# A fused attention and feed-forward kernel: ScalarE's and TensorE's order at the seam behind each feed-forward stage is rewritten

## The reference

```python
xh = layernorm(x)
u = einsum(q, k) * scale / sqrt(16)          # q from xh, k and v from ctx, by head
p = softmax(where(mask, -inf, tanh(u) * exp(log_C)))
x = x + (p @ v) @ W_out.T
out = layernorm(x); gf = global_net(out.mean over tokens)     # 256 -> 128 -> 64 -> 1
for _ in range(3):
    tf = sigmoid(gelu(gelu(gelu(out @ w1 + b1) @ w2 + b2) @ w3 + b3) @ w4 + b4)
    coupling = 0.1 + adaptive_range * (0.7 * gf + 0.3 * tf - 0.5) * 2
    out = out + coupling * twist(out)        # twist permutes quarters of the features, with signs
x = x + out
```

## Time and profile before

| | us |
|---|---|
| median of 3 runs | 1056.2 (1056.09 to 1056.72) |
| the profiled execution: its own time | 1056.83 |
| its span, first to last instruction | 1055.0 |
| from one seam to the next (token_tanh at 296.65 and 421.77) | 125.1 |
| TensorE, ScalarE, VectorE, GpSimd busy | 972.8, 902.8, 819.0, 603.8 |

### The profile page before, as it was taken

The page is one execution under the profiler, slowest core; times in us unless marked ns, Lnnn a source line. Parts: engine busy times, 40 slices in busy tenths (PEclk is TensorE's granted clock), DMA queues, the critical chain, the costliest instruction groups (busy, mean ns, idle before and its releaser), DMA issues.

```text
span 1055.0 us, 21747 instructions
## 1 busy us (share of the span) xinstructions
PE 972.8 (92%) x7260; PEld 529.1 (50%) x7260; DVE 819.0 (78%) x1655; ACT 902.8 (86%) x1121; POOL 603.8 (57%) x1077
## 2 busy tenths in 40 slices
PE   5899999999999999999999999999999999997994
PEld 4556535564356544565445653556435654454431
DVE  3888785997869876887859978599786987687475
ACT  3899878997899978998789988899789997896575
POOL 3366715887069850898328980588706975087204
PEclk7999999999999999999999999999999999999897
DMA  5433001540024300332005310154002430021002
GB/s 119 89 60 60 6 2 31 117 90 1 2 69 91 78 1 1 90 93 56 2 1 119 89 30 1 32 117 90 0 2 70 94 75 1 1 52 37 8 1 81
DMA packets 191117, 51.70 MB, mean 49 GB/s; under 512 B 165920, under 2 KB 174624, under 8 KB 191008
## 3 DMA queue, kind: packets, MB, share of 16 engines
q1 hardware_dynamic: 191008, 50.31, 22.5%
HBM read 33.37 MB, written 16.78 MB: 48 GB/s over the span
## 4 chain that ended last, share of the span: by engine, by line
PE 41%; ACT 36%; issue 10%; DVE 8%; POOL 3%; SPq 2%; DMA 0%; ACTq 0%; DVEq 0%; POOLq 0%
ACT probs L939 17%; ACT probs L945 13%; PE ps L1295 11%; PE ps L1281 8%; PE ps L1265 6%; ACT f_t L955 4%; PE ps L1304 4%; PE ps L1185 4%; PE ps L1216 3%; DVE move_u L802 2%; DVE move_v L804 2%; PE ps L1201 2%; DVE f_t L808 2%; PE ps L1325 1%; SPq L412 1%
## 5 line engine op out<-in xcount | busy, mean ns | idle before, releaser
L939 ACT ACTIVATE probs<-ps,u_scale 120x2048 f32<-120x2048 f32 x128 | 258.0, 2016 | 23.0 <-PE ps L1185 23.0
L945 ACT ACTIVATE probs<-probs,exp_bias,clip 120x2048 f32<-120x2048 f32 x128 | 275.6, 2153 | 0.1
L1295 PE MATMUL ps<-h,w 128*128 128x512 f32 x384 | 186.9, 609 | 1.7 <-ACT h L973 1.7
L1185 PE MATMUL ps<-q_t,k_t 32*120 32x256 f32 x2048 | 148.3, 403 | 26.7 <-ACT probs L939 25.9
L717 DVE STREAM_TRANSPOSE o_t<-ps 128x512 f32<-128x512 f32 x128 | 90.6, 708 | 73.6 <-PE ps L1201 73.4
L1216 PE MATMUL ps<-wo_t,of_t 128*128 128x256 f32 x512 | 143.5, 403 | 1.0 <-DVE xy L742 1.0
L1201 PE MATMUL ps<-probs,va 120*32 120x256 f32 x2048 | 138.8, 389 | 1.3 <-ACT probs L945 1.3
L498 POOL TENSOR_SCALAR tok_c<-tok_c,c_tok 128x32 f32<-128x32 f32 x8 | 2.3, 288 | 237.7 <-issue 237.7
L1185 PEld LDWEIGHTS ps<-q_t,k_t 32*120 32x120 f32 x2048 | 93.8, 179 | 63.8 <-issue 59.5
L973 ACT ACTIVATE h<-f_t,b 128x512 f32<-128x512 f32 x144 | 96.9, 718 | 18.0 <-DVE f_t L827 13.5
L1216 PEld LDWEIGHTS ps<-wo_t,of_t 128*128 128x128 f32 x512 | 86.9, 189 | 50.0 <-issue 41.7
(11 more groups left out here) (138 smaller groups left out, 1765.5 us busy)
## 6 DMA issues: line engine op xcount, KB each, us to landing
xy<-in_x_dram SPq DMA_DIRECT2D x64, 256.0 KB, 3.4
out_dram<-xy SPq DMA_DIRECT2D x64, 256.0 KB, 2.0
cbuf<-in_ctx_dram SPq DMA_DIRECT2D x64, 120.0 KB, 2.8
va<-in_ctx_dram SPq DMA_DIRECT2D x64, 120.0 KB, 3.6
tok_c<-coup SPq DMA_DIRECT2D x256, 0.5 KB, 2.0
move_v<-in_L_xattn_W_out_dram SPq DMA_DIRECT2D x1, 256.0 KB, 5.1
move_u<-in_L_ffn_cn_w_dram SPq DMA_DIRECT2D x1, 256.0 KB, 3.1
w<-in_L_ffn_cn_w_dram SPq DMA_DIRECT2D x1, 128.0 KB, 3.0
```

What stands on the lines that cost most here:

```text
L939: eng.activation(probs[:, b % 2, n * HALF:(n + 1) * HALF, :].rearrange("k h q -> k (h q)"), banks(SCORE_BANK, 4)[0:KEYS, :], ACT.Tanh, sca ...
L945: eng.activation(p, p, ACT.Exp, scale=clip[0:KEYS, 0:1], bias=exp_bias[:, b:b + 1]).then_inc(s_exp, 1)
L1185: last = eng.matmul(banks(SCORE_BANK + r)[0:KEYS, odd * S:(odd + 1) * S], k_t[rows, b % 2, odd, n, :], q_t[rows, b % 2, n, :], start=True, ...
L1295: last = eng.matmul(banks(bank), w2[:, k, :], h1[:, p % 2, k, :], start=(k == 0), stop=(k == EK - 1))
```

## The change

1. On TensorE norm_to_features(24) moves from slot 27 into the ffn loop (p = 11), to `SIDE_BANK`; scores(27, 1) moves one step later, behind layer3(11); token_output(10) moves behind it, and token_output writes `X_BANK`. weighted_values(26, 0) leaves the ffn loop for slot 27.
2. TensorE's slot 27 becomes queries(28), weighted_values(26, 0), keys(28), project(25, 0), scores(28, 0), weighted_values(26, 1), project(25, 1). Slot 28 no longer begins with scores(28, 0).
3. ScalarE's order becomes gelu2(11), gelu3(10), features(24), gelu3(11), tanh(27, 1), token_tanh, exp(27, 0), and slot 28 as before.
4. VectorE does queries_out(28) ahead of attn_out(26, 0).
5. queries(28) waits for the last gelu3 in place of token_tanh; project(25, 0) waits for token_tanh in place of the last wide tanh.

In the last group, behind which no attention follows, only the order of token_output(10) and layer3(11), and the bank of the token outputs, change.

```diff
@@ vector
+                    if after_ffn(i) and nxt < NB:
+                        queries_out(nxt)
                     if 0 <= here < NB:
                         attn_out(here, 0)
-                    if 0 <= nxt < NB:
+                    if 0 <= nxt < NB and not after_ffn(i):
                         queries_out(nxt)
@@ scalar, attention slot
-                    if 0 <= i - LAG < NB:
-                        features(i - LAG)
+                    if 0 <= i - LAG < NB and not first:
+                        features(i - LAG, TR_BANK)
@@ scalar, ffn loop
-                            if early < NB and p >= PASSES - 2 and p < PASSES:
-                                tanh(early, p - PASSES + 2)
+                            if early < NB:
+                                if p == PASSES - 2:
+                                    tanh(early, 0)
+                                if p == PASSES - 1:
+                                    features(early - LAG, SIDE_BANK)
+                                if p == PASSES:
+                                    tanh(early, 1)
@@ tensor, queries(b)
                 elif after_ffn(b - 1):
-                    eng.wait_ge(s_ttok, groups_before(b - 1))
+                    eng.wait_ge(s_h3, PASSES * groups_before(b - 1))
@@ tensor, project(b, 0)
                     if after_ffn(b + 2):
-                        eng.wait_ge(s_th, UPDATES * groups_before(b + 2))
+                        eng.wait_ge(s_ttok, groups_before(b + 2))
@@ tensor, norm_to_features(b, bank)
-                if nxt < NB:
+                if bank == SIDE_BANK:
+                    eng.wait_ge(s_h2, PASSES * groups_before(b + LAG))
+                elif nxt < NB:
                     eng.wait_ge(s_kt, nxt + 1)
@@ tensor, attention slot
                     if i != early:
-                        if 0 <= i < NB:
+                        if 0 <= i < NB and i - 1 != early:
                             scores(i, 0)
...
                     else:
-                        if old < NB:
-                            project(old, 0)
-                        if nxt < NB:
-                            queries(nxt)
-                        if here < NB:
-                            weighted_values(here, 1)
-                    if 0 <= nxt < NB:
+                        queries(nxt)
+                        weighted_values(here, 0)
                         keys(nxt)
-                    if 0 <= here < NB and i != early:
+                        project(old, 0)
+                        scores(nxt, 0)
                         weighted_values(here, 1)
-                    if 0 <= old < NB:
                         project(old, 1)
-                    if 0 <= i - LAG < NB:
-                        norm_to_features(i - LAG)
@@ tensor, ffn loop
-                        if p - 2 >= UPDATES:
+                        if p - 2 >= UPDATES and p < PASSES:
                             token_output(i, p - 2)
...
                             if p == PASSES - 2:
                                 scores(early, 0)
                             if p == PASSES - 1:
+                                norm_to_features(early - LAG, SIDE_BANK)
+                            if p == PASSES:
                                 scores(early, 1)
-                            if p == PASSES:
-                                weighted_values(early - 1, 0)
+                        if p >= PASSES:
+                            token_output(i, p - 2)
```

More of the change, by code:

```diff
@@ L199, in xattn_ffn_kernel @@
         SMALL_AT = S
-        TOKEN_AT = S + 32
+        TOKEN_BANK = X_BANK
         L4_BANK = X_BANK
@@ L945, in exp, with features @@
                 eng.activation(p, p, ACT.Exp, scale=clip[0:KEYS, 0:1], bias=exp_bias[:, b:b + 1]).then_inc(s_exp, 1)
-            def features(b):
+            def features(b, bank):
                 eng.wait_ge(s_ftr, b + 1)
@@ L954, in features @@
                 for k in range(EK):
-                    eng.activation(f_t[:, k, at * S:(at + 1) * S], banks(TR_BANK)[:, k * S:(k + 1) * S],
+                    eng.activation(f_t[:, k, at * S:(at + 1) * S], banks(bank)[:, k * S:(k + 1) * S],
                                    ACT.Identity, scale=F_SCALE, accum_out=f_sum[:, k, at:at + 1]).then_inc(s_ft, 1)
@@ L1026, in token_tanh @@
                 eng.wait_ge(s_coef, COEFS * g)
-                eng.activation(tok_th[:], banks(TR_BANK)[:, TOKEN_AT:TOKEN_AT + GT], ACT.Tanh, scale=0.5,
+                eng.activation(tok_th[:], banks(TOKEN_BANK)[:, 0:GT], ACT.Tanh, scale=0.5,
                                bias=half_b4[:, 0:1]).then_inc(s_ttok, 1)
@@ L1218, in project, with norm_to_features @@
                 last.then_inc(s_proj, 1)
-            def norm_to_features(b):
+            def norm_to_features(b, bank):
                 eng.wait_ge(s_fhat, 2 * (b + 1))
                 nxt = b + LAG + 1
-                if nxt < NB:
+                if bank == SIDE_BANK:
+                    eng.wait_ge(s_h2, PASSES * groups_before(b + LAG))
+                elif nxt < NB:
                     eng.wait_ge(s_kt, nxt + 1)
@@ L1228, in norm_to_features @@
                     for t in range(TT):
-                        last = eng.transpose(banks(TR_BANK)[:, k * S + t * P:k * S + (t + 1) * P],
+                        last = eng.transpose(banks(bank)[:, k * S + t * P:k * S + (t + 1) * P],
                                              f_hat[:, t, k * P:(k + 1) * P], ident[:])
@@ L1333, in token_output @@
                 for t in range(TT):
-                    at = TOKEN_AT + t * GROUP + chunk * CB
-                    last = eng.matmul(banks(TR_BANK)[:, at:at + CB], h3[:, p % 2, t * P:(t + 1) * P],
+                    at = t * GROUP + chunk * CB
+                    last = eng.matmul(banks(TOKEN_BANK)[:, at:at + CB], h3[:, p % 2, t * P:(t + 1) * P],
                                       w4rep[:, :, 0], start=True, stop=True)
@@ L1372, in _ @@
                             project(old, 0)
-                    else:
-                        if old < NB:
-                            project(old, 0)
-                        if nxt < NB:
-                            queries(nxt)
-                        if here < NB:
-                            weighted_values(here, 1)
-                    if 0 <= nxt < NB:
+                        if 0 <= nxt < NB:
+                            keys(nxt)
+                        if 0 <= here < NB:
+                            weighted_values(here, 1)
+                        if 0 <= old < NB:
+                            project(old, 1)
+                        if 0 <= i - LAG < NB:
+                            norm_to_features(i - LAG, TR_BANK)
+                    else:
+                        queries(nxt)
+                        weighted_values(here, 0)
                         keys(nxt)
-                    if 0 <= here < NB and i != early:
+                        project(old, 0)
+                        scores(nxt, 0)
                         weighted_values(here, 1)
-                    if 0 <= old < NB:
                         project(old, 1)
-                    if 0 <= i - LAG < NB:
-                        norm_to_features(i - LAG)
                     if i == 0:
```

## The result

| | before | after |
|---|---|---|
| median of 4 runs | 1056.46 us (1056.09 to 1057.07) | 1061.95 us (1061.55 to 1062.25) |
| ratio after / before | | 1.0051, 95% interval 1.0034 to 1.0069 |
| the profiled execution: own time, span | 1056.83, 1055.0 | 1062.25, 1060.5 |
| mean distance of token_tanh from seam to seam, first to seventh | 125.23 us | 126.08 us |

The kernel is 5.5 us slower; the forecast was 1061.7 with a range of 1056.0 to 1063.3. In the trace 0.85 us a seam are lost: (928.68 - 172.20) / 6 = 126.08 after, (922.73 - 171.38) / 6 = 125.23 before.

A forecast was written before the change was run, and what follows sets the result against it. Each seam was taken as bound by ScalarE and, 0.14 us behind, by the work behind attn_out (26, 1). Seven seams at +0.86, less 0.5, gave +5.5 us: 1061.7, range 1056.0 to 1063.3.

The forecast's parts named there:

- The slack of 0.14 and the double bound: At each seam before: ScalarE sets tanh (29, 0), and the path behind attn_out (26, 1) follows only 0.14 us behind.
- The end of the ffn loop is worth nothing: Reordering up to token_tanh gains nothing: it comes at 421.82 against 421.77, with features(24) between gelus needing no table load.
- tanh (28, 0) gains 1.70: On ScalarE behind exp (27, 0): tanh (28, 0) starts at 425.40 in place of 427.10, 1.70 us earlier.
- D = 1.00: Delay of attn_out (26, 1) on VectorE, from a sum of nine steps: start at 426.11 in place of 425.11.
- The same 6.07 us behind it: VectorE's work from attn_out (26, 1) to the end of queries_out(29) stays 6.07 us, with nothing taken out.
- +0.86 a seam: tanh (29, 0) starts at 436.36 instead of 435.50, so each of seven seams costs 0.86 us more.
- -0.5 at the end: In the last group layer3(11) starts at 1038.01 in place of 1038.54, so the end comes 0.53 us sooner, once.
- The sum: Whole kernel: 7 x 0.86 = 6.0, less 0.5, is +5.5 us.
- ScalarE's pace: Rival: ScalarE alone decides at the seams, so 12.4 us are won, 1043.8; 13 in 100.
- the two meet: Rival: D is only 0.1 to 0.4, a seam moves nothing to +0.26, 1055.5 to 1057.5; 11 in 100.

The follow-up runs named there:

- experiment 4: Kernel before, with four of the eight heads of exp (27, 1) left out at each seam: 1055.25 us, ratio 0.9991.
- experiment 6: Kernel before, with the combine of slot 27 moved behind queries_out(29) on VectorE: 1056.48 us, ratio 1.0000.
- Experiment 7: Changed kernel with VectorE's old order in slot 27, attn_out (26, 0) ahead of queries_out(28): 1076.20 us, ratio 1.0183 to the kernel before.
- experiment 1: Changed kernel with weighted_values (26, 1) ahead of scores (28, 0) on TensorE: 1054.09 us, ratio 0.9979 to the kernel before.
- experiment 2: Changed kernel with the combine of slot 27 moved behind queries_out(29) on VectorE: 1057.32 us, ratio 1.0014 to the kernel before.
- experiment 5: Changed kernel with both weighted_values (26, 1) ahead of scores (28, 0) and the combine of slot 27 behind queries_out(29): 1049.31 us, ratio 0.9931 to the kernel before.
- experiment 3: Changed kernel with four of the eight heads of exp (27, 1) left out at each seam: 1063.93 us, ratio 1.0067 to the kernel before.
- experiment 8: Kernel before, with only the last group's layer3(11) ahead of token_output(10) and its token outputs in bank 7: 1055.11 us, single run.

## Why the prediction was right

**The slack of 0.14 and the double bound.** The slack is right: in experiment 4 tanh (29, 0) came 0.14 sooner, and experiment 6 won nothing from VectorE's 0.66. The bound was not double but threefold. "TensorE runs without a gap" was read only from keys(29) on, but it holds from scores (28, 1) on, and experiment 6 puts TensorE's own queue 0.07 us behind VectorE. For this change that made no difference, since VectorE came nearly 1 us later and TensorE then waited 1.64 us.

**The end of the ffn loop is worth nothing.** Right: token_tanh starts 424.32 - 420.56 = 3.76 behind the end of gelu3(10); it was forecast at 3.70 and was 3.65 before. features(24) took its place between the gelus with no table load: the only one of the seam stands ahead of exp. The Trainium skill (ScalarE: Activation LUTs, Table sets: the hidden batching unit) has identity in every set, and this trace agrees. The same page's 2.66 us for a switch (What ACT_TABLE_LOAD costs) is not seen: exp starts 1.31 behind token_tanh's end, the load of 1.28 included.

**tanh (28, 0) gains 1.70.** It gained 1.64.

**D = 1.00.** attn_out (26, 1) starts at 428.50 - 2.44 = 426.06, 0.95 later than before. The sum of nine steps was 0.05 too long. VectorE's idle time ahead of it was forecast at 2.3 and is 2.31.

**The same 6.07 us behind it.** 6.20 at this seam, 6.10 to 6.20 at the seven: divide's product took 0.81 here in place of 0.69. The bounds had allowed 0.2. Experiment 7, where this product took 0.69, has 6.07 again. What lengthened it was not tried.

**+0.86 a seam.** 0.94 at the seam shown, 0.85 as the mean of the six distances, 126.08 where 126.0 was forecast. At the seam shown it is 0.95 + 0.13 - 0.14: the two small errors of the terms, -0.05 and +0.13, partly cancel. Experiments 1, 2 and 5 show that it is this path, and experiment 3 that it isn't ScalarE, whose 0.39 + 1.61 + 0.26 = 2.26 us of waits were forecast as about 2.5.

**-0.5 at the end.** The step is worth that (experiment 8), but in the changed kernel's own profile it is 1043.12 to 1045.82, 2.70 against 2.93, so only -0.23: its token products took 1.50 us together, with a mean granted clock of 0.87 in this stretch, against 1.24 at 1.00 in experiment 8. It is too small for the sum to depend on it.

**The sum.** The spans of the two profiled executions differ by the forecast 5.5, and that closeness is partly luck. In the changed kernel's the first token_tanh comes 0.82 us later, of which the change explains 0.11 (3.76 for 3.65); and from the seventh seam to the last token_tanh it takes 117.14 in place of 117.68, where the seam's 0.85 less 0.23 would have made it 118.3. These +0.7 and -1.2 nearly cancel. What makes them was not tried. The first token_tanh lies at 171.26 to 171.53 in the four profiles with the order of before and at 171.33 to 172.77 in the six with the new one, so this part may be scatter or a cost of the change that no term had. The last stretch scatters: experiment 8, with 0.49 less to do there, took 1.81 less, 115.87. What is shown without such luck is the 0.85 between seams. (The range's upper end, 1063.3, is 0.2 above the 1063.1 of its own sum.)

**The rivals.** "ScalarE's pace" fell with experiment 3, and "the two meet" with the measured D. The rule of the Trainium skill beside the first of these (Perfetto Trace Analysis, Identifying the Most-Contended Engine) would have looked at ScalarE, the fullest engine of the stretch before; the trace disagrees about this seam, where VectorE, 0.38 us less full, decided as soon as its chain was started late.

## What to carry to other kernels

Where an engine is full, look at which other engines have no wait in the same stretch: the slack between them, here 0.14 us to the second and 0.07 more to the third, is all that a better order of the first can win before another one decides. When an instruction is moved ahead of others in a queue, ask what hangs on the ones pushed back: scores (28, 0) came when ScalarE wanted them, but they pushed weighted_values (26, 1) back, and VectorE's full chain behind those started 0.95 us later. All of that delay but the 0.14 of slack was lost. A loss of this kind may be one exchange away from a win: with weighted_values ahead of the scores the same change is 2.3 us faster than the kernel before, and with the combine moved as well 7.2 us.

## What was not expected of the hardware

The same wait of 1.5 us on TensorE lowered its clock at some seams and not at others. In experiment 7 keys(28) waited 1.50 or 1.51 us at all seven. At the seams of 301, 428, 685 and 941 us the granted clock stayed at 1.00. At those of 171, 556 and 812 it fell to 0.50, in the wait (171) or at its end (556, 812), and came back 3 to 7 us later; the projection's four matmuls took 1.93 us there in place of 1.03. In the 14.6 us or so behind token_tanh the mean granted clock was 0.77, 0.88 and 0.88. The changed kernel, whose TensorE waits 1.64 us for keys(29) at the seam of 424 (1.54 at 172), shows 1.00 in the 15 us behind each of its seven seams. What makes the difference was not tried. The drops cost experiment 7 some 6 us beside the 8.4 of its seven seams.
